# Two convolution-style layers over a 512 x 512 x 128 tensor: products of the first projection one group later, and one reciprocal moved behind a scaling in the second

## The chip, the cores and the metric

The kernel runs on one core of one Trainium2 chip. The metric is the device time of one execution in microseconds (us); lower is better.

## What is computed

The input `x` has 512 x 512 positions of 128 channels in float32. Two layers follow each other, each added to its own input. Cut to what matters here:

```
x = x + L0(group_norm(x))
    a = sigmoid((x @ Wa1 + ba1) * (x @ Wa2 + ba2))      # 16 channels
    b = sigmoid((x @ Wb1 + bb1) * (x @ Wb2 + bb2))      # 16 channels
    z = einsum('bikc,bkjc->bijc', a, b)
    L0 = sigmoid(x @ Wg + bg) * (layer_norm(z) @ Wz + bz)
x = x + L1(group_norm(x))
    xn = layer_norm(x)
    h = (xn @ pi_w.T + pi_b) * sigmoid(xn @ gi_w.T + gi_b) * mask
    a1, b1, a2, b2 = split(h)
    y = concat(einsum('bikd,bjkd->bijd', a1, b1), einsum('bkid,bkjd->bijd', a2, b2))
    L1 = (layer_norm(y) @ po_w.T + po_b) * sigmoid(layer_norm(y) @ go_w.T + go_b)
```

## The kernel before, in words

The program has seven stages that run one after the other; between two stages all engines meet. Stage 1 gathers the statistics of the first group norm, stage 2 computes `a` and `b`, stage 3 multiplies them, stage 4 makes layer 0's output and the second group norm's statistics, stage 5 computes `h`, stage 6 the two products of layer 1, stage 7 its output. The change touches stages 2 and 5.

Every engine has its own written-out order of instructions, and semaphores tie the orders together. No scheduler moves anything: what stands ahead in an engine's order runs ahead.

**Stage 2, the first projection** (`stage2_gates`, lines 388 to 571). The 512 rows of `x` are worked in 128 groups of four rows (1 MB each). Six group buffers are filled ahead by DMA (`load`, line 382). For each group g:

- TensorE turns it, in two halves h of two rows: `turn(r, g, h)`, eight 128 x 128 transposes into one of three slots of `x_ps` (line 454).
- ScalarE scales a half by the group norm and rounds it to fp16: `round_high` writes `high` (line 498). VectorE computes what the rounding left: `rest` writes `low` (line 548). A slot of `x_ps` is free again once `rest` has read it.
- TensorE multiplies with the weights, split in fp16 parts: `product(r, g, m)`, twelve matmuls of 32 x 512 for m = 0 (the first factor) and twelve for m = 1 (the second), into `p_ps[:, m]` (line 467). It waits for both halves of `rest` of its group.
- ScalarE adds the bias to the first factor: `open_first` (line 504). VectorE multiplies in the second: `multiply` writes `gate` (line 555). ScalarE applies the sigmoid: `sigmoid` writes `ab` (line 511). `p_ps` has one buffer for each m, so `product(g, 0)` waits for `open_first(g-1)` and `product(g, 1)` for `multiply(g-1)`.

In one step of the loop, TensorE does turn(g+2, 0), product(g+1, 0), turn(g+2, 1), product(g+1, 1); ScalarE does sigmoid(g), round_high(g+3, 0), open_first(g+2), round_high(g+3, 1); VectorE does multiply(g), rest(g+2, 0), rest(g+2, 1). A body of the loop has six steps, one for each group buffer.

The SP queue issues both loads and stores of this stage: six `reload(r, k)`, each once buffer k has been turned (line 417), and then two `store` of 768 KB, each once the sigmoids of three groups are done (line 421). The second store waits for the sixth sigmoid of the body, and the next body's first load stands behind it in the queue.

**Stage 5, the second projection** (`stage5_project`, lines 995 to 1299). Pairs n of rows are worked, sixteen in a body; eight pairs are a block, whose layer-norm deviations are computed together. For each pair TensorE spreads the reciprocal deviations (`spread_scale`, line 1259), multiplies for the gate and for the projection (`project`, line 1268) and turns the pair n+12 (`turn`, line 1243). VectorE does `scale(n+2)` (line 1194), `statistics(n+11)` (line 1172) and `gate_h(n)` (line 1201). Once in a block ScalarE computes the deviations (`deviation`, line 1084, after pair 4 of the block; it loads an activation table ahead and another after), VectorE inverts them (`invert`, line 1178, in the step of pair 5) and splits the result in two fp16 parts (`split_high`, `split_low`, lines 1183 and 1187), TensorE turns these (`turn_parts`, line 1250), and ScalarE copies the result out (`keep_rows`, line 1089), which the next block's first `spread_scale` needs. The two split steps wait for the reciprocal and for each other by the semaphore `chain`.

Of the kernel before, what the change touches and what calls it, by code (L numbers as in the profile page):

```python
# [387 lines left out]
def stage2_gates(nc, K, ahead, ab_d, N):  # L388
# [11 lines left out]
    with ExitStack() as stack:  # L400
# [12 lines left out]
        def _(block):  # L413
# [25 lines left out]
            @block.tensor  # L439
            def _(pe):  # L440
                for m in range(2):
                    pe.matmul(p_ps[:, m, 0:1], K.Wab4[:, m, :], K.gn_shift[:], start=True, stop=True).then_inc(shifted, 1)
                pe.wait_ge(folded, 2)
                pe.sem_inc(done, 2 * GROUPS)

                def turn(r, g, h):

                    k, n = g % GROUPS, (2 * g + h) % SLOTS
                    if h == 0:
                        pe.wait_ge(loaded[k], (r + g // GROUPS) * 16 + 16)  # L450
                    pe.wait_ge(rest_ready, r * PAIRS + (2 * g + h + 1))
                    for j in range(2):
                        for q in range(CB):
                            last = pe.transpose(x_ps[:, n, j, q * P:(q + 1) * P], xt[:, k, 2 * h + j, q, :], K.ident[:])  # L454
                    last.then_inc(turned, 1)

                def product(r, g, m):
                    pe.wait_ge(rest_ready, r * PAIRS + (2 * g + 2 + SLOTS))
                    if m == 0:
                        pe.wait_ge(opened, r * GROUPS + (g + 1))  # L460
                    else:
                        pe.wait_ge(gated, r * GROUPS + (g + 2))
                    half = slice(32 * m, 32 * m + 32)
                    for weights, part, start, stop in ((K.Wab_high, high, True, False), (K.Wab_low, high, False, False),
                                                       (K.Wab_high, low, False, True)):
                        for j in range(U):
                            last = pe.matmul(p_ps[32 * j:32 * j + 32, m, 0:N], weights[:, half], part[:, g % GROUPS, j, :],
                                             start=start, stop=stop)
                    last.then_inc(done, 1)

                def step(r, g, end=None):
                    for h in range(2):
                        if end is None or g + 2 < end:
                            turn(r, g + 2, h)
                        if end is None or g + 1 < end:
                            product(r, g + 1, h)

                for g in range(2):
                    for h in range(2):
                        turn(0, g, h)  # L480
                for m in range(2):
                    product(0, 0, m)
                with pe.Fori(0, REPS - 1) as r:
                    for g in range(GROUPS):
                        step(r, g)
                for g in range(TAIL):
                    step(REPS - 1, g, TAIL)

            @block.scalar
            def _(act):  # L490
                act.sem_inc(sig, 2)
                act.sem_inc(opened, 1)

                def round_high(r, g, h):
                    act.wait_ge(turned, r * PAIRS + (2 * g + h + 1))
                    if h == 0:
                        act.wait_ge(done, r * PAIRS + (2 * g + 2))
                    act.activation(high[:, g % GROUPS, 2 * h:2 * h + 2, :], x_ps[:, (2 * g + h) % SLOTS, :, 0:N], ACT.Copy,  # L498
                                   scale=K.gn_scale[:]).then_inc(rounded, 1)

                def open_first(r, g):
                    act.wait_ge(done, r * PAIRS + (2 * g + 1 + 2 * GROUPS))
                    act.wait_ge(gated, r * GROUPS + (g + 1))
                    act.activation(first[:, g % 2, :], p_ps[:, 0, 0:N], ACT.Identity, bias=bias[:, 0:1]).then_inc(opened, 1)

                def sigmoid(r, g):
                    k = g % GROUPS
                    act.wait_ge(gated, r * GROUPS + (g + 1 + 2))
                    if k % 3 == 0:
                        act.wait_ge(stored[k // 3], (r + g // GROUPS) * 16 + 16)  # L510
                    act.activation(ab[:, k // 3, k % 3, :], gate[:, g % 2, :], ACT.Sigmoid).then_inc(sig, 1)

                def step(r, g, end=None):
                    sigmoid(r, g)
                    if end is None or g + 3 < end:
                        round_high(r, g + 3, 0)
                    if end is None or g + 2 < end:
                        open_first(r, g + 2)
                    if end is None or g + 3 < end:
                        round_high(r, g + 3, 1)  # L520

                for g in range(2):
                    for h in range(2):
                        round_high(0, g, h)
                act.wait_ge(folded, 2)
                open_first(0, 0)
                round_high(0, 2, 0)
                open_first(0, 1)
                round_high(0, 2, 1)
                act.activation(bias_gate[:], K.bg[:], ACT.Sigmoid)  # L530
                with act.Fori(0, REPS - 1) as r:
                    for g in range(GROUPS):
                        step(r, g)
                for g in range(TAIL):
                    step(REPS - 1, g, TAIL)

            @block.vector
            def _(dve):
                dve.sem_inc(rest_ready, SLOTS)
                dve.sem_inc(gated, 2)  # L540
                for m in range(2):
                    dve.wait_ge(shifted, m + 1)
                    dve.tensor_tensor(bias[:, m:m + 1], p_ps[:, m, 0:1], K.bias4[:, m:m + 1], ALU.add).then_inc(folded, 1)
                dve.wait_ge(folded, 2)

                def rest(r, g, h):
                    dve.wait_ge(rounded, r * PAIRS + (2 * g + h + 1))
                    dve.scalar_tensor_tensor(low[:, g % GROUPS, 2 * h:2 * h + 2, :], x_ps[:, (2 * g + h) % SLOTS, :, 0:N], K.gn_scale[:],  # L548
                                             high[:, g % GROUPS, 2 * h:2 * h + 2, :], ALU.mult, ALU.subtract).then_inc(rest_ready, 1)

                def multiply(r, g):
                    dve.wait_ge(done, r * PAIRS + (2 * g + 2 + 2 * GROUPS))
                    dve.wait_ge(opened, r * GROUPS + (g + 2))
                    dve.wait_ge(sig, r * GROUPS + (g + 1))
                    dve.scalar_tensor_tensor(gate[:, g % 2, :], p_ps[:, 1, 0:N], bias[:, 1:2], first[:, g % 2, :],
                                             ALU.add, ALU.mult).then_inc(gated, 1)

                def step(r, g, end=None):
                    multiply(r, g)
                    if end is None or g + 2 < end:  # L560
                        for h in range(2):
                            rest(r, g + 2, h)

                for g in range(2):
                    for h in range(2):
                        rest(0, g, h)
                with dve.Fori(0, REPS - 1) as r:
                    for g in range(GROUPS):
                        step(r, g)
                for g in range(TAIL):  # L570
                    step(REPS - 1, g, TAIL)

def stage3_triangle(nc, K, ab_d, z_d, N):
# [420 lines left out]
def stage5_project(nc, K, ahead, mask, mask_d, h_d, N):  # L995
# [9 lines left out]
    with ExitStack() as stack:  # L1005
# [27 lines left out]
        def _(block):  # L1033
# [127 lines left out]
            def _(dve):  # L1161
# [14 lines left out]
                def invert(r, b):  # L1176
                    dve.wait_ge(dev_ready, r * 2 + (b + 1))
                    dve.reciprocal(rstd[:], dev[:]).then_inc(chain, 1)
# [24 lines left out]

                def step(r, n, last=False):
                    chained = not (last and n + 3 >= PAIRS)
                    if n % BLOCK == 5 and chained:
                        invert(r, (n + 3) // BLOCK)
                    if not (last and n + 2 >= PAIRS):
                        scale(r, n + 2)
                    if n % BLOCK == 5 and chained:  # L1210
                        split_high(r, (n + 3) // BLOCK)
                        split_low(r, (n + 3) // BLOCK)
                    if not (last and n + LEAD - 1 >= PAIRS):
                        statistics(r, n + LEAD - 1)
                    gate_h(r, n)
# [627 lines left out]
```

## Time and profile before

| what | value |
|---|---|
| median of 3 runs | 4825.3 us (4824.75 to 4827.78) |
| the profiled execution, its own time | 4827.47 us |
| its span, first to last instruction | 4825.7 us |
| mean granted TensorE clock | 0.975 |
| busy: PE, DVE, ACT, POOL | 3997.2, 3925.1, 3395.2, 2674.1 us |
| stage 2: first turn to last sigmoid | 373.9 to 939.3 us |
| stage 5: first turn to last scaling | 2062 to 3142 us |

PE is TensorE's matmuls, PEld its weight loads, DVE VectorE, ACT ScalarE, POOL GpSimd, SPq the queue on which SyncE issues DMAs. A row of a timeline gives start, duration, engine, line, operation, output <- input, and in square brackets how long the engine had been idle before it and what ended that. The busy share of a whole span averages over seven stages with different limits, so it does not say what limits stage 2 or stage 5. Only short stretches inside a stage do.

### The profile page before, as it was taken

The numbers are of one execution on the slowest core, as the hardware profiler recorded it, in microseconds if no ns is written. First come the engines' busy times: TensorE is split into PE (matmuls) and PEld (weight loads), VectorE is DVE, ScalarE is ACT, GpSimd is POOL, SyncE is SP. The second block draws the span as 40 slices with busy tenths as digits, with TensorE's granted clock in tenths as the row PEclk, the third lists the DMA queues.
The fourth block names the chain that finished last, engine by engine and source line by source line (L and its number), as shares of the span: only waits on it lengthen the run. The fifth ranks groups of instructions, "written<-read, shape, count | busy, mean of one in ns | idle before, by whom it ended". The sixth has DMA issues, their size and how long they took to land. (4 is left out here: it accounts for less than half of the span.)

```text
span 4825.7 us, 89597 instructions
## 1 busy us (share of the span) xinstructions
PE 3997.2 (83%) x26438; PEld 2240.6 (46%) x26438; DVE 3925.1 (81%) x5450; ACT 3395.2 (70%) x4840; POOL 2674.1 (55%) x1428
## 2 busy tenths in 40 slices
PE   0007888795599999889999999979999978888888
PEld 0004444452366666545555555545554434444444
DVE  5787777678888888989999999867779987777777
ACT  2337777654577777768888888746667768888887
POOL 0000000085488888757778777843334418888887
PEclk9999999997799999989999999999999989999999
DMA  9997888753999999969999999876679869999999
GB/s 367 416 385 247 296 299 301 241 175 105 307 399 390 390 391 391 393 215 316 315 315 318 311 313 318 276 263 222 224 237 308 302 213 362 407 405 404 402 404 362
DMA packets 700625, 1532.70 MB, mean 318 GB/s; under 512 B 32976, under 2 KB 50832, under 8 KB 698128
## 3 DMA queue, kind: packets, MB, share of 16 engines
q1 hardware_dynamic: 563696, 1263.31, 73.0%
q10 hardware_dynamic: 136864, 268.59, 14.5%
q8 instruction: 33, 0.54, 0.0%
q14 instruction: 32, 0.26, 0.0%
HBM read 1009.59 MB, written 522.19 MB: 317 GB/s over the span
## 5 line engine op out<-in xcount | busy, mean ns | idle before, releaser
L1762 POOL TENSOR_TENSOR s_oT<-s_gated,s7in_x1t 128x1024 f32<-128x1024 f32 x256 | 689.4, 2699 | 218.5 <-DVE s_gated L1681 213.6
L976 POOL TENSOR_TENSOR s_x1T<-s_gz,s_xT 128x512 f32<-128x512 f32 x512 | 653.4, 1276 | 126.6 <-DVE s_gz L942 122.0
L1428 PE MATMUL s_y_ps<-s_ab 128*128 128x512 f16 x3072 | 678.4, 379 | 1.8 <-DVE s_ab L1499 1.8
L1133 POOL TENSOR_TENSOR s_low<-s_xc,s_high 128x1024 f16<-128x1024 f32 x256 | 547.8, 2140 | 237.4 <-ACT s_high L1094 235.9
L873 PE MATMUL s_g_ps<-s_xT,s_Wg 128*128 128x512 f32 x1024 | 523.3, 593 | 0.0
L713 POOL MEMSET s_total<- 128x2048 f32 x1 | 1.8, 1810 | 936.2 <-POOLq L41 936.2
L903 ACT ACTIVATE s_g<-s_g_ps,s_bg 128x512 f32<-128x512 f32 x512 | 352.0, 688 | 173.1 <-PE s_g_ps L873 173.1
L1681 DVE SCALAR_TENSOR_TENSOR s_gated<-s_p_ps,k_po_bias,s_gate 128x1024 f32<-128x1024 f32 x256 | 328.7, 1284 | 177.2 <-ACT s_gate L1718 145.7
L1428 PEld LDWEIGHTS s_y_ps<-s_ab 128*128 128x128 f16 x3072 | 300.4, 98 | 343.4 <-issue 2.0
L548 DVE SCALAR_TENSOR_TENSOR s_low<-s_x_ps,k_gn_scale,s_high 128x1024 f16<-128x1024 f32 x256 | 328.5, 1284 | 161.0 <-ACT s_high L498 160.9
L942 DVE SCALAR_TENSOR_TENSOR s_gz<-s_z_ps,k_z_bias,s_g 128x512 f32<-128x512 f32 x512 | 384.4, 751 | 88.8 <-ACT s_g L903 86.6
L1099 ACT ACTIVATE s_gate<-s_g_ps,k_gi_bias 128x1024 f32<-128x1024 f32 x256 | 284.3, 1110 | 200.7 <-PE s_g_ps L1268 200.4
L1402 POOL TENSOR_TENSOR s_at<-s_at,s_mask 128x1024 f32<-128x1024 f32 x64 | 151.1, 2360 | 460.6 <-DMA s_bt<-h_d 265.6
L1718 ACT ACTIVATE s_gate<-s_g_ps,k_go_bias 128x1024 f32<-128x1024 f32 x256 | 286.0, 1117 | 148.0 <-PE s_g_ps L1627 134.8
L863 PEld LDWEIGHTS s_x_ps<-k_ident,s_xt 128*128 128x128 f32 x2048 | 257.1, 141 | 274.8 <-issue 268.3
L1172 DVE BATCH_NORM_STATS2 s_stats<-s_x_ps 128x6 f32<-128x256 f32 x1024 | 364.1, 418 | 7.8 <-PE s_x_ps L1243 7.1
L1201 DVE SCALAR_TENSOR_TENSOR s_h<-s_p_ps,k_pi_bias,s_gate 128x1024 f32<-128x1024 f32 x256 | 328.2, 1282 | 46.8 <-PE s_p_ps L1268 32.2
L933 DVE BATCH_NORM_STATS2 s_stats<-s_x1T 128x512 f32 (+1 forms) x512 | 349.8, 683 | 0.2 <-POOL s_x1T L976 0.2
L498 ACT ACTIVATE s_high<-s_x_ps,k_gn_scale 128x1024 f16<-128x1024 f32 x256 | 285.2, 1114 | 74.3 <-PE s_x_ps L454 73.6
L307 DVE BATCH_NORM_STATS2 s_stats<-s_xt 128x512 f32 x416 | 248.5, 682 | 81.1 <-DMA s_xt<-in_x 81.1
L863 PE MATMUL s_x_ps<-k_ident,s_xt 128*128 128x128 f32 x2048 | 308.5, 274 | 6.5 <-DVE s_bg L929 6.5
L1194 DVE TENSOR_TENSOR s_xc<-s5in_xt,s_r_ps 128x1024 f32<-128x1024 f32 x256 | 310.2, 1212 | 4.3 <-PE s_r_ps L1259 3.0
(225 smaller groups left out, 9506.7 us busy)
## 6 DMA issues: line engine op xcount, KB each, us to landing
s2in_xt<-in_x SPq DMA_DIRECT2D x128, 1024.0 KB, 8.5
s_xt<-in_x SPq DMA_DIRECT2D x256, 512.0 KB, 8.4
x_d<-s_x1T ACTq DMA_DIRECT2D x128, 1024.0 KB, 9.6
s5in_xt<-x_d SPq DMA_DIRECT2D x128, 1024.0 KB, 9.2
h_d<-s_h SPq DMA_DIRECT2D x128, 1024.0 KB, 6.9
s7in_x1t<-x_d SPq DMA_DIRECT2D x128, 1024.0 KB, 14.0
out<-s_ot ACTq DMA_DIRECT2D x128, 1024.0 KB, 9.3
s_mask_b<-mask_d SPq DMA_DIRECT2D x128, 512.0 KB, 4.8
```

Of the source, the lines that this page charges most:

```text
L548: dve.scalar_tensor_tensor(low[:, g % GROUPS, 2 * h:2 * h + 2, :], x_ps[:, (2 * g + h) % SLOTS, :, 0:N], K.gn_scale[:], high[:, g % GROUPS ...
L863: last = pe.transpose(x_ps[:, i % 4, q * P:(q + 1) * P], xt[:, i // U, i % U, q, :], K.ident[:])
L873: pe.matmul(g_ps[:, i % 2, 0:N], Wg[:], xT[:, i % 8, :], start=True, stop=True).then_inc(g_prod, 1)
L903: act.activation(g[:, i % 2, :], g_ps[:, i % 2, 0:N], ACT.Sigmoid, bias=bg[:]).then_inc(sig, 1)
L933: dve.bn_stats(stats[:, bass.ds(r * ROWS + i, 1), :].rearrange("p a s -> p (a s)"), x1T[:, i // U, i % U, :]).then_inc(counted, 1)
L942: dve.scalar_tensor_tensor(gz[:, i % 4, :], z_ps[:, i % 2, 0:N], K.z_bias[:], g[:, i % 2, :], ALU.add, ALU.mult).then_inc(mixed, 1)
L976: pool.tensor_tensor(x1T[:, i // U, i % U, :], gz[:, i % 4, :], xT[:, i % 8, :], ALU.add).then_inc(added, 1)
L1133: pool.tensor_tensor(low[:, n % 4, :, :], xc[:, n % 4, :, :], high[:, n % 4, :, :], ALU.subtract).then_inc(rest_ready, 1)
L1172: last = dve.bn_stats(stats[:, row // 16 % 2, row % 2, row // 2 % BLOCK, a, :], x_ps[:, row % 2, 2 * a * P:(2 * a + 2) * P].rearrange("p ( ...
L1428: last = pe.matmul(y_ps[:, ib, 0:N], ab[:, u % 2, 0, a, kb, ib * P:(ib + 1) * P], ab[:, u % 2, 1, b, kb, :], start=m == 0, stop=m == len(t ...
L1681: dve.scalar_tensor_tensor(gated[:, n % 4, :, :], p_ps[:], K.po_bias[:], gate[:, n % 2, :, :], ALU.add, ALU.mult).then_inc(mixed, 1)
L1762: pool.tensor_tensor(oT[:, n % 4, :, :], gated[:, n % 4, :, :], x1t[:, n // 2, 2 * (n % 2):2 * (n % 2) + 2, :], ALU.add).then_inc(added, 1)
```

## The change

It has two parts.

In stage 2, TensorE's step becomes turn(g+2, 0), product(g, 0), turn(g+2, 1), product(g, 1): the products belong to a group that is two behind the turned one and not one behind. ScalarE's step becomes round_high(g+2, 0), open_first(g), round_high(g+2, 1), sigmoid(g-1), and VectorE's multiply(g-1), rest(g+2, 0), rest(g+2, 1). The first body of ScalarE and VectorE is written out ahead of their loops, since it has no sigmoid or multiply of an earlier body. The SP queue's order of loads and stores is unchanged.

In stage 5, VectorE does `scale(n+2)` ahead of `invert` in the step of pair 5 of a block, where it did it after.

```diff
@@ stage 2, TensorE
                     for h in range(2):
                         if end is None or g + 2 < end:
                             turn(r, g + 2, h)
-                        if end is None or g + 1 < end:
-                            product(r, g + 1, h)
+                        product(r, g, h)
...
-                for m in range(2):
-                    product(0, 0, m)
@@ stage 2, ScalarE
-                def step(r, g, end=None):
-                    sigmoid(r, g)
-                    if end is None or g + 3 < end:
-                        round_high(r, g + 3, 0)
-                    if end is None or g + 2 < end:
-                        open_first(r, g + 2)
-                    if end is None or g + 3 < end:
-                        round_high(r, g + 3, 1)
+                def step(r, g, first=False, end=None):
+                    ahead = end is None or g + 2 < end
+                    if ahead:
+                        round_high(r, g + 2, 0)
+                    open_first(r, g)
+                    if ahead:
+                        round_high(r, g + 2, 1)
+                    if g:
+                        sigmoid(r, g - 1)
+                    elif not first:
+                        sigmoid(r - 1, GROUPS - 1)
@@ stage 2, VectorE
-                def step(r, g, end=None):
-                    multiply(r, g)
+                def step(r, g, first=False, end=None):
+                    if g:
+                        multiply(r, g - 1)
+                    elif not first:
+                        multiply(r - 1, GROUPS - 1)
                     if end is None or g + 2 < end:
                         for h in range(2):
                             rest(r, g + 2, h)
@@ stage 5, VectorE
-                    if n % BLOCK == 5 and chained:
-                        invert(r, (n + 3) // BLOCK)
                     if not (last and n + 2 >= PAIRS):
                         scale(r, n + 2)
                     if n % BLOCK == 5 and chained:
+                        invert(r, (n + 3) // BLOCK)
                         split_high(r, (n + 3) // BLOCK)
                         split_low(r, (n + 3) // BLOCK)
```

The order of the instructions shows it at three places. On TensorE (the start of stage 2), the 32 transposes of the first two groups stood ahead of the products of group 0, and then came the loop:

```order
 L454 MATMUL s_x_ps<-k_ident,s2in_xt 128x128 x32
-L467 MATMUL s_p_ps<-s_high,k_Wab_high 32x512 x4
-L467 MATMUL s_p_ps<-s_high,k_Wab_low 32x512 x4
-L467 MATMUL s_p_ps<-s_low,k_Wab_high 32x512 x4
-L467 MATMUL s_p_ps<-s_high,k_Wab_high 32x512 x4
-L467 MATMUL s_p_ps<-s_high,k_Wab_low 32x512 x4
-L467 MATMUL s_p_ps<-s_low,k_Wab_high 32x512 x4
-L483 UNCONDITIONAL_BRANCH
```

These six rows of products are gone from there. The loop's rows read the same as before (eight transposes, twelve matmuls, eight transposes, twelve matmuls), but the first twelve matmuls in it are now group 0's and not group 1's.

On ScalarE, one step of the loop in stage 2 (`s_ab` is the sigmoid's output, `s_high` the rounded half, `s_first` the first factor) stood before as

```order
L511 ACTIVATE s_ab<-s_gate 128x512
L495 REGISTER_ALU
L497 REGISTER_ALU
L498 ACTIVATE s_high<-s_x_ps,k_gn_scale 128x1024
L502 REGISTER_ALU
L504 ACTIVATE s_first<-s_p_ps,s_bias 128x512
L498 ACTIVATE s_high<-s_x_ps,k_gn_scale 128x1024
```

and stands now as

```order
L494 REGISTER_ALU
L495 ACTIVATE s_high<-s_x_ps,k_gn_scale 128x1024
L499 REGISTER_ALU
L501 ACTIVATE s_first<-s_p_ps,s_bias 128x512
L495 ACTIVATE s_high<-s_x_ps,k_gn_scale 128x1024
L505 REGISTER_ALU
L508 ACTIVATE s_ab<-s_gate 128x512
```

The sigmoid has moved from the head of a step to its end.

On VectorE in stage 5, in the step of pair 5 of a block (`s_xc` is the scaled pair, `s_rstd` the reciprocal, `s_parts` its two parts, `s_h` the gated projection of the pair before), the order was

```order
L1201 SCALAR_TENSOR_TENSOR s_h<-s_p_ps,k_pi_bias,s_gate 128x1024
L1177 ISA
L1178 RECIPROCAL s_rstd<-s_dev 128x64
L1194 TENSOR_TENSOR s_xc<-s5in_xt,s_r_ps 128x1024
L1181 ISA
L1183 TENSOR_SCALAR s_parts<-s_rstd 128x2x32
L1186 REGISTER_ALU
L1187 SCALAR_TENSOR_TENSOR s_parts<-s_rstd,s_parts 128x2x32
```

and is now

```order
L1206 SCALAR_TENSOR_TENSOR s_h<-s_p_ps,k_pi_bias,s_gate 128x1024
L1199 TENSOR_TENSOR s_xc<-s5in_xt,s_r_ps 128x1024
L1182 ISA
L1183 RECIPROCAL s_rstd<-s_dev 128x64
L1186 ISA
L1188 TENSOR_SCALAR s_parts<-s_rstd 128x2x32
L1191 REGISTER_ALU
L1192 SCALAR_TENSOR_TENSOR s_parts<-s_rstd,s_parts 128x2x32
```

The scaling, which stood between the reciprocal and the first split, stands ahead of both.

## Rows read from the trace of the kernel before

**Rows 1.** Timeline, stage 2: one step's rows on TensorE, ScalarE and VectorE.

```profile
704.33 1.09 PE L454 MATMUL s_x_ps<-k_ident,s2in_xt 128*128 128x128 f32 x8
...
705.46 1.11 ACT L498 ACTIVATE s_high<-s_x_ps,k_gn_scale 128x1024 f16<-128x1024 f32 x1 [0.32 <-PE s_x_ps L454]
...
706.12 1.09 PE L454 MATMUL s_x_ps<-k_ident,s2in_xt 128*128 128x128 f32 x8
...
706.61 1.28 DVE L548 SCALAR_TENSOR_TENSOR s_low<-s_x_ps,k_gn_scale,s_high 128x1024 f16<-128x1024 f32 x1 [1.23 <-ACT s_high L498]
...
707.81 0.74 DVE L555 SCALAR_TENSOR_TENSOR s_gate<-s_p_ps,s_bias,s_first 128x512 f32<-128x512 f32 x1
...
707.95 0.40 PE L467 MATMUL s_p_ps<-s_high,k_Wab_high 128*32 128x512 f16 x4 [0.74 <-DVE s_low L548]
...
708.71 1.09 PE L454 MATMUL s_x_ps<-k_ident,s2in_xt 128*128 128x128 f32 x8
```

**Rows 2.** Timeline, ScalarE at the start of stage 2, where it worked without a wait.

```profile
387.11 0.62 ACT L511 ACTIVATE s_ab<-s_gate 128x512 f32<-128x512 f32 x1
...
390.20 0.63 ACT L511 ACTIVATE s_ab<-s_gate 128x512 f32<-128x512 f32 x1
```

**Rows 3.** Busy time in stretches of stage 2: start:end, length, engines, clock, DMA share, GB/s.

```profile
699.40:722.20 22.80, 19.10 (x215) 11.30 (x208) 16.56 (x17) 17.62 (x22) 0.00 (x0) 1.00 0.99 343
...
705.00:715.00 10.00, 8.52 (x97) 4.88 (x96) 6.67 (x7) 7.80 (x10) 0.00 (x0) 1.00 1.05 392
699.40:725.75 26.35, 21.83 (x244) 13.02 (x240) 18.88 (x19) 20.62 (x25) 0.00 (x0) 1.00 0.86 298
```

**Rows 4.** The same view, a stretch of stage 4.

```profile
1500.00:1550.00 50.00, 50.00 (x233) 31.28 (x232) 44.72 (x67) 38.96 (x67) 42.24 (x34) 1.00 1.04 392
```

**Rows 5.** Timeline, the SP queue in stage 2: three of its load issues.

```profile
709.99 0.37 SPq L382 DMA_DIRECT2D s2in_xt<-in_x  x1
...
714.37 0.37 SPq L382 DMA_DIRECT2D s2in_xt<-in_x  x1
...
725.83 0.40 SPq L382 DMA_DIRECT2D s2in_xt<-in_x  x1
```

**Rows 6.** DMA issues on the page: count, size, median us from issue to landing.

```profile
s2in_xt<-in_x SPq DMA_DIRECT2D x128, 1024.0 KB, 8.5
```

**Rows 7.** Timeline, stage 5: the step with the reciprocal and the next.

```profile
2611.34 0.38 ACT L1084 ACTIVATE s_dev<-s_stats,s_eps 128x64 f32<-128x64 f32 x1
...
2611.75 0.55 DVE L1178 RECIPROCAL s_rstd<-s_dev 128x64 f32<-128x64 f32 x1 [1.20 <-ACT s_dev L1084]
...
2612.22 1.16 DVE L1194 TENSOR_TENSOR s_xc<-s5in_xt,s_r_ps 128x1024 f32<-128x1024 f32 x1
...
2613.30 0.18 DVE L1183 TENSOR_SCALAR s_parts<-s_rstd 128x64 f16<-128x64 f32 x1
...
2613.87 0.23 PE L1250 MATMUL s_r_ps<-k_ident_h,s_parts 128*128 128x128 f16 x1 [0.79 <-DVE s_parts L1187]
2614.05 1.05 ACT L1094 ACTIVATE s_high<-s_xc 128x1024 f16<-128x1024 f32 x1
...
2614.99 0.27 ACT L1089 ACTIVATE s_rows<-s_r_ps 128x128 f16<-128x128 f16 x1
...
2615.72 0.40 PE L1259 MATMUL s_r_ps<-s_rows,s_select 64*128 64x128 f16 x8
...
2616.19 1.22 DVE L1194 TENSOR_TENSOR s_xc<-s5in_xt,s_r_ps 128x1024 f32<-128x1024 f32 x1
...
2620.09 1.22 DVE L1194 TENSOR_TENSOR s_xc<-s5in_xt,s_r_ps 128x1024 f32<-128x1024 f32 x1
```

**Rows 8.** Timeline, stage 5, another block: the turned parts and the next two scalings.

```profile
2314.99 0.23 PE L1250 MATMUL s_r_ps<-k_ident_h,s_parts 128*128 128x128 f16 x1 [1.06 <-DVE s_parts L1187]
...
2317.31 1.22 DVE L1194 TENSOR_TENSOR s_xc<-s5in_xt,s_r_ps 128x1024 f32<-128x1024 f32 x1
...
2322.85 1.22 DVE L1194 TENSOR_TENSOR s_xc<-s5in_xt,s_r_ps 128x1024 f32<-128x1024 f32 x1
```

**Rows 9.** Busy time in a stretch of that block, columns as in Rows 3.

```profile
2317.00:2321.00 4.00, 4.00 (x19) 1.47 (x16) 2.87 (x6) 2.41 (x3) 3.74 (x2) 0.57 0.86 317
```

More of the change, by code:

```diff
@@ L525, in _ @@
                 act.wait_ge(folded, 2)
[L526 to L529, printed above, removed]
                 act.activation(bias_gate[:], K.bg[:], ACT.Sigmoid)
-                with act.Fori(0, REPS - 1) as r:
+                for g in range(GROUPS):
+                    step(0, g, first=True)
+                with act.Fori(1, REPS - 1) as r:
                     for g in range(GROUPS):
@@ L534, in _ @@
                 for g in range(TAIL):
-                    step(REPS - 1, g, TAIL)
+                    step(REPS - 1, g, end=TAIL)
+                sigmoid(REPS - 1, TAIL - 1)
             @block.vector
@@ L566, in _ @@
                         rest(0, g, h)
-                with dve.Fori(0, REPS - 1) as r:
+                for g in range(GROUPS):
+                    step(0, g, first=True)
+                with dve.Fori(1, REPS - 1) as r:
                     for g in range(GROUPS):
@@ L570, in _ @@
                 for g in range(TAIL):
-                    step(REPS - 1, g, TAIL)
+                    step(REPS - 1, g, end=TAIL)
+                multiply(REPS - 1, TAIL - 1)
 def stage3_triangle(nc, K, ab_d, z_d, N):
```

## The prediction

> **What bounds the kernel now.** The page's shares average over seven stages, so I read stretches inside the two stages that the change touches: first the table of busy time, then the timeline, then the queue of the loads.
>
> Stage 2 first. In 26.35 us, one body of six groups, no engine is full: TensorE is busy 21.83 us, ScalarE 20.62, VectorE 18.88, and the DMA engines have a share of 0.86 at a granted clock of 1.00 [rows 3]. A group takes 26.35 / 6 = 4.39 us. Where nothing is full, a loop of waits sets the pace, and the timeline shows it [rows 1]. The second half of a group is turned at 704.33; ScalarE rounds it from 705.46 (1.13 later); VectorE computes the rest from 706.61 (1.15 later); the group's first product waits for just that rest and starts at 707.95 (1.34 later, TensorE idle for 0.74); behind that product the next second half is turned, at 708.71 (0.76 later). 1.13 + 1.15 + 1.34 + 0.76 = 4.38 us, the whole period. So stage 2 is bound by one loop through three engines, closed by the product that stands ahead of the next turn.
>
> Stage 5: a normal step takes 2620.09 - 2616.19 = 3.90 us from scaling to scaling. The step with the reciprocal is longer: from that step's scaling to the next is 2616.19 - 2612.22 = 3.97, but VectorE was idle for 1.20 us ahead of the reciprocal, waiting for ScalarE's deviations, with a scaling that needed nothing behind it, and TensorE idled for 0.79 until the parts were split [rows 7].
>
> **The change, stage 2.** Nothing is added or removed in the work; the same transposes, matmuls, activations and VectorE operations run in another order. A product now needs the rest of a group that was turned a whole step earlier, so the loop above is open. What is next?
>
> - TensorE by itself: a turn and a product take 706.12 - 704.33 = 1.79 us from start to start [rows 1], a group has two of each: 3.57 us.
> - ScalarE: from one sigmoid to the next without a wait 390.20 - 387.11 = 3.09 us [rows 2].
> - VectorE: two rests of 1.20 (706.61 to 707.81) and a multiply of at most 0.74 [rows 1]: 3.14 us.
> - A new loop, over two groups: turn(g+2, 1), rounding, rest; VectorE does multiply(g) behind that rest; product(g+1, 1) waits for it; behind it stand turn(g+4, 0), product(g+2, 0) and the next turn. 1.13 + 1.15 + 1.20 + 0.80 + 0.76 + 1.03 + 0.76 = 6.83 us for two groups, 3.42 for one. It lies 0.31 us over two groups below TensorE's own pace, so it doesn't decide.
> - DMA: a body loads six groups and stores twice 768 KB. The share adds up to 0.99 x 22.80 = 22.6 us of all engines, in a stretch of 22.80 us; the 3.55 us behind it are idle. Where loads alone stand in line the share is 1.05 [rows 3]. If stores and loads fill the engines as well as that, as stage 4 does with loads and stores mixed (1.04 at 392 GB/s [rows 4]), the body needs 22.6 / 1.05 = 21.5 us, 3.59 for a group. If the stretch can't be packed any tighter than it is, it needs 22.8 us, 3.80 for a group.
>
> So the next limit is the DMA between 3.59 and 3.80 us, with TensorE at 3.57 just below. The stores run worse than the loads now, partly since the queue runs dry around them; a closed queue should mend some of it. I take 3.70, the middle, since neither row is nearer. The gain is 4.39 - 3.70 = 0.69 us a group. Of the 128 groups the last two have no turn ahead of them and drain at nearly the old pace, so 126 count: **87 us**. The ends of this term are 126 x (4.39 - 3.80) = 74 and 126 x (4.39 - 3.57) = 103. Filling and draining the pipe by one more group costs at most one product pair, 2 x 0.76 = 1.5 us, and I leave it in the range.
>
> The SP queue is the one that the move lengthens. Its second store waits for the body's sixth sigmoid, which now comes one step later after the turn, and the next body's first load stands behind that store. Buffer 0 of the next body is turned one period behind 714.37, at 718.75 (issues of free buffers come 4.38 apart), and its load is issued at 725.83, 7.1 us later [rows 5]. With 3.70 us a step that becomes about 10.8. The buffer is wanted again six steps after it was free, 22.2 us, so 11.4 us are left for the landing, against a median of 8.5 [rows 6]. It fits, with little to spare, so I cost this at nothing; it is covered only while a landing stays below 11 us.
>
> **Stage 5.** VectorE's scaling fills the 1.20 us of idleness. The reciprocal can't start sooner than 2611.75, since ScalarE's deviation ends then. Behind it the first split needs its result: 0.55 and a semaphore of about 0.07, so it starts at 2612.37 and not at 2613.30, 0.93 us sooner, and the turned parts on TensorE with it. But not all of this reaches the end. The next spreading on TensorE (2615.72) needs ScalarE's copy of the rows, and ScalarE is not early: table, gate and rounding run there without a gap to 2614.99, where the copy starts with no wait [rows 7]. It ends at 2615.26, so the spreading can start at 2615.30, 0.42 us sooner. From there TensorE and VectorE go on at 3.90 a step, TensorE without a gap. 31 blocks pass here (32 reciprocals, one ahead of the loop): 31 x 0.42 = **13 us**. The ends are 31 x 0.93 = 29, if the copy of the rows weren't a brake, and 0, if ScalarE's wait only moves.
>
> **The sum.** 87 + 13 = 100 us off the profiled execution's 4827.5 gives 4727.5. That execution lies 2.2 us above the median, so the forecast is **4725 us**, 2.1% less. Changes within 0.2% (10 us) can hardly be told from none here.
>
> **The rivals.**
> - *TensorE is the bound* (DMA packs to 3.57 or better): 103 + 13, 4709 us. For: 3.59 if loads and stores fill the engines like stage 4. Against: each body's first load is issued late. Chance 0.20.
> - *The DMA can't be packed tighter*: 3.80 a group, 74 + 10, 4741 us. For: stores run at a lower rate than loads whatever stands behind them. Chance 0.18.
> - *The clock falls once in every body*: with 3.70 us of DMA against 3.57 of TensorE, 6 x 0.13 = 0.8 us of waiting collect in front of one turn. At 1.64 us for each of 21 bodies, all of it on the path: 34 us given back, 4759 us. Against: a late TensorE has DMA slack to catch up with. Chance 0.05. This is what the rule above would make of it.
> - *The order doesn't open the loop*: something on ScalarE, whose open_first(g) stands ahead of round_high(g+2, 1), delays the rounding as before; the two-group loop would have to grow from 6.83 to 8.78 us. Then only stage 5 gains: 4812 us. Chance 0.03.
> - *Slower*: the late second store starves the loads. It decides where a body's first load lands more than 6 x 4.39 - (7.1 + 4.4) = 14.8 us after its issue. If landings double to 17 us the body takes 17 + 11.5 = 28.5 us, 4.75 a group: 126 x 0.36 = 45 us more, less 13, 4857 us. Against: the landing of 8.5 us is already that of a queue with three in line. Chance 0.04.
>
> **How the numbers follow.** The forecast's own case, 3.62 to 3.78 a group, has 0.50. The low end takes in TensorE as the bound and some of stage 5's upper end (4709 less 9), the high end the rival on the clock: 4700 to 4762. All of stage 2's better cases lie in it; outside are the last two and a stage 2 worse than 3.85, about 0.12. Faster by over 0.2% are the first three and the forecast, 0.94 with the share of the fourth that is below 4815; slower 0.04; within 0.2% 0.02.
>
> **What would show it.** In the profile after, a stretch of six groups in stage 2 should last 22.2 us, with a DMA share above 1.0 and no idle stretch, the product's wait for the rest gone and instead one wait a body for a load on TensorE. TensorE at 3.57 with DMA share below 1.0 would speak for the first rival, a share near 0.99 at 22.8 for the second, a granted clock below 1.00 in stage 2 for the third. In stage 5 the wait ahead of the reciprocal should shrink to almost nothing, the one for the split parts too, and the copy of the rows should be what the spreading waits for. A stage 2 above 4.2 us a group, or a stage 5 that isn't shorter, would make the reasoning wrong.

## The result, and the profile after

The changed kernel takes 4711.9 us (median of 4 runs, 4710.5 to 4714.6), the kernel before 4826.0 in the same comparison: a ratio of 0.9762, 95% interval 0.9750 to 0.9775, so 2.4% or 114 us less. The forecast was 4725 us with a range of 4700 to 4762. The direction and the range hold; the time is that of the first rival (4709 us), TensorE as the bound of stage 2.

| | before | after | difference |
|---|---|---|---|
| the profiled execution, its own time | 4827.5 | 4714.6 | -112.9 |
| span | 4825.7 | 4712.9 | -112.8 |
| stage 2, first to last sigmoid | 387.1 to 938.7 | 391.1 to 840.1 | -102.6 |
| stage 5, first to last scaling | 2087.1 to 3140.7 | 1988.0 to 3024.3 | -17.3 |

The two stages account for 119.9 us; the rest moved by 7 us the other way. 3.5 us of it lie ahead of stage 2's first turn (at 373.9 us before and 377.4 after), in a stage that the change doesn't touch, and 3.6 us behind stage 5. The kernel with only stage 5 changed (below) has its first turn at 377.3 too, so the first part belongs to the executions and not to the change.

Stage 2 in the busy-time view of the profile after, columns as in [rows 3]: one body of the loop, from a first load's issue to the next body's.

```profile
647.02:668.44 21.42, 21.42 (x243) 13.01 (x242) 18.88 (x19) 19.95 (x25) 0.00 (x0) 1.00 1.02 367
```

A body takes 21.42 us and not 26.35, a group 3.57. TensorE is busy in all of it (this view counts as busy the 0.1 to 0.2 us between two kinds of matmuls that are looked at below), the clock is at 1.00 and the DMA engines have a share of 1.02 at 367 GB/s. The timeline of one step, TensorE and VectorE and ScalarE, answers to [rows 1]:

```profile
700.16 1.09 PE L454 MATMUL s_x_ps<-k_ident,s2in_xt 128*128 128x128 f32 x8
...
700.73 1.28 DVE L547 SCALAR_TENSOR_TENSOR s_low<-s_x_ps,k_gn_scale,s_high 128x1024 f16<-128x1024 f32 x1
...
701.18 0.40 PE L467 MATMUL s_p_ps<-s_high,k_Wab_high 128*32 128x512 f16 x4
...
701.94 1.09 PE L454 MATMUL s_x_ps<-k_ident,s2in_xt 128*128 128x128 f32 x8
...
702.44 1.28 DVE L547 SCALAR_TENSOR_TENSOR s_low<-s_x_ps,k_gn_scale,s_high 128x1024 f16<-128x1024 f32 x1 [0.42 <-ACT s_high L495]
...
702.97 0.40 PE L467 MATMUL s_p_ps<-s_high,k_Wab_high 128*32 128x512 f16 x4
...
703.73 1.09 PE L454 MATMUL s_x_ps<-k_ident,s2in_xt 128*128 128x128 f32 x8
```

From turn to turn of the same half 703.73 - 700.16 = 3.57 us. The products at 701.18 and 702.97 follow their turns with no wait; the 0.74 us ahead of the first product in [rows 1] are gone, and VectorE's wait for the rounding is 0.42 us where it was 1.23.

The load issues of the SP queue answer to [rows 5], and the landing on the page to [rows 6]:

```profile
656.68 11.11 SPq L422 DMA_DIRECT2D ab_d<-s_ab  x2
668.44 8.63 SPq L382 DMA_DIRECT2D s2in_xt<-in_x  x6
```

```profile
s2in_xt<-in_x SPq DMA_DIRECT2D x128, 1024.0 KB, 9.6
```

A merged row runs from its first issue to its last. The six loads of a body are now issued within 8.6 us, and a load of this stage lands 9.6 us after its issue in the median (8.5 before). The first of them is the one that its buffer waits for longest. The sixth goes out as soon as its own buffer is turned, at 676.3; the first buffer was turned five groups of 3.57 us earlier, so the load at 668.44 is issued some 10 us after its buffer came free. TensorE has no wait for a load in the waits of this stretch, so this late issue is covered.

Stage 5, the step with the reciprocal, answers to [rows 7]:

```profile
2405.69 1.21 DVE L1199 TENSOR_TENSOR s_xc<-s5in_xt,s_r_ps 128x1024 f32<-128x1024 f32 x1
...
2406.97 0.55 DVE L1183 RECIPROCAL s_rstd<-s_dev 128x64 f32<-128x64 f32 x1
...
2407.56 0.43 DVE L1188 TENSOR_SCALAR s_parts<-s_rstd 128x64 f16<-128x64 f32 x1
...
2408.38 0.23 PE L1254 MATMUL s_r_ps<-k_ident_h,s_parts 128*128 128x128 f16 x1
...
2409.26 1.05 ACT L1099 ACTIVATE s_high<-s_xc 128x1024 f16<-128x1024 f32 x1
...
2410.21 0.27 ACT L1094 ACTIVATE s_rows<-s_r_ps 128x128 f16<-128x128 f16 x1
...
2410.53 0.40 PE L1263 MATMUL s_r_ps<-s_rows,s_select 64*128 64x128 f16 x8 [0.23 <-ACT s_rows L1094]
2439.59 0.55 DVE L1183 RECIPROCAL s_rstd<-s_dev 128x64 f32<-128x64 f32 x1
```

The scaling runs where VectorE was idle, and the reciprocal starts with no wait as soon as the deviations are there. From it to the turned parts are 1.41 us (2.12 before), but the spreading that begins the next block now waits for ScalarE's copy of the rows, which stands behind the rounding as it did. This block takes 2439.59 - 2406.97 = 32.62 us, as most do; the mean from 2080.56 to 2831.79 is 32.66, over 23 blocks. Before, a block without a fall of the clock took 33.03 (reciprocals at 2611.75 and 2644.78 in the trace of before).

### The profile page after: what moved, and what is told of

Read it like the earlier page. It is cut to its first block and busy times, and to the rows that moved or that the text cites. A ratio compares the mean times of both kernels' runs of the same rounds, so it can differ in the third digit from the quotient of the medians.

```text
span 4712.9 us, 89415 instructions
## 1 busy us (share of the span) xinstructions
PE 3987.0 (85%) x26438; PEld 2239.9 (48%) x26438; DVE 3935.2 (83%) x5450; ACT 3377.8 (72%) x4840; POOL 2670.3 (57%) x1428
## 5 line engine op out<-in xcount | busy, mean ns | idle before, releaser
L1199 DVE TENSOR_TENSOR s_xc<-s5in_xt,s_r_ps 128x1024 f32<-128x1024 f32 x256 | 311.7, 1218 | 10.8 <-PE s_r_ps L1263 9.6
```

## The experiments

Eight more kernels ran, three of them once only: the two with fewer products and the one with the sigmoid at the head. The comparisons with the kernel before were made in three sets, in which its own median was 4826.0, 4828.1 and 4829.6 us, so differences between sets are good to some 4 us.

**One part of the change at a time.** Stage 5's edit undone:

```diff
+                    if n % BLOCK == 5 and chained:
+                        invert(r, (n + 3) // BLOCK)
                     if not (last and n + 2 >= PAIRS):
                         scale(r, n + 2)
                     if n % BLOCK == 5 and chained:
-                        invert(r, (n + 3) // BLOCK)
                         split_high(r, (n + 3) // BLOCK)
```

> The changed kernel with stage 5's scaling put back behind the reciprocal. If the two parts add up as the stages' lengths in the two traces say (stage 2 102 us shorter, stage 5 17 us shorter), it takes 4826 - 102 = 4724 us, a group of stage 2 takes 3.57 us, and stage 5's blocks take 33.03 us again, with a wait of 1.2 us ahead of each reciprocal and again a few falls of the clock. If stage 5's gain came from somewhere else (less heat or another phase after a shorter stage 2), it stays near 4712 us.

Measured: 4728.3 us, a ratio of 0.9791 (0.9776 to 0.9806), 99.8 us less than before and 4 more than expected. Stage 2 is as in the changed kernel (448.9 us from first to last sigmoid, 449.0 there). The waits of the middle of stage 5 in this kernel's trace (engine, line, waited for, total us, times, longest):

```profile
DVE s_rstd L1183 <- ACT s_dev L1089: 33.5, 28, 1.2
PE s_r_ps L1255 <- DVE s_parts L1192: 21.8, 28, 0.8
```

The 1.2 us ahead of each reciprocal are back, 28 times, and blocks take 33.02 us again. But the granted clock was 1.00 through all of the middle of stage 5: the falls of [rows 8, 9] did not come back with the wait. TensorE's wait was at most 0.8 us here. In the trace of before, the three blocks with a fall were those where it had waited longer, 1.06, 1.27 and 1.17 us, and the others had 0.76 to 0.79.

The other half alone, the kernel before with only stage 5's edit:

```diff
-                    if n % BLOCK == 5 and chained:
-                        invert(r, (n + 3) // BLOCK)
                     if not (last and n + 2 >= PAIRS):
                         scale(r, n + 2)
                     if n % BLOCK == 5 and chained:
+                        invert(r, (n + 3) // BLOCK)
                         split_high(r, (n + 3) // BLOCK)
```

> The kernel before with only stage 5's scaling moved ahead of the reciprocal. Theory (ScalarE's copy of the rows limits a block to 0.41 us of gain, and the three falls of the clock at 1.6 us each vanish with the wait): 31 x 0.41 + 5 = 18 us less, 4808 us, blocks of 32.62 us, granted clock 1.00 in the middle of stage 5. Rival (the falls of the clock are chance and come back): 13 us less, 4813 us, with clock below 1.00 in some blocks.

Measured: 4815.6 us, a ratio of 0.9974 (0.9964 to 0.9984), 12.5 us less. The rival's number, 31 x 0.41 = 13, is the right one: the 5 us of the three falls are not in the difference of the medians. The traces agree. From first to last scaling, stage 5 took 1053.6 us in the trace of before, with three falls, but 1048.6 and 1049.6 us with the same order of stage 5 in the kernel with only stage 2 changed (no fall) and in the kernel before with fewer products (one fall); with the new order it is 1037.5 us here and 1036.3 in the changed kernel. How many falls the other executions of the kernel before had, no trace shows. There was no fall in this trace's middle either, so what the rival said of the clock did not show. The two halves add: 99.8 + 12.5 = 112.3 us, against 114 for both.

**Which loop bound stage 2 before.** The kernel before with the third of a product's matmul passes left out. The low part of the input is then computed and not multiplied.

```diff
-                    for weights, part, start, stop in ((K.Wab_high, high, True, False), (K.Wab_low, high, False, False),
-                                                       (K.Wab_high, low, False, True)):
+                    for weights, part, start, stop in ((K.Wab_high, high, True, False), (K.Wab_low, high, False, True)):
```

> The kernel before with the same third matmul pass left out in stage 2. Theory of one loop through turn, rounding, rest and the first product: only one of the two products lies in the loop, so the group falls by 0.215 us, from 4.39 to 4.17: 28 us less, 4798 us. Rival, TensorE's own pace sets the period with waits as a by-product: it falls by 0.43, 55 us less, 4771 us. Rival, the DMA sets it: no change.

Measured: 4802.3 us, 25.8 less than before. First to last sigmoid took 524.7 us where it took 551.6: 26.9 us over 127 groups, 0.21 a group. TensorE lost 0.43 us of work in a group and the group got 0.21 shorter: one product lies in the loop, the other beside it. That is the loop of the prediction, and neither rival. The run cut both products at once; that it is the first one that lies in the loop is read from [rows 1], where TensorE waits ahead of that one.

**What is next in stage 2: TensorE or the DMA.** The same edit on the changed kernel.

> The changed kernel with the third of the three matmul passes of a product in stage 2 left out (the low part of the input is computed but not multiplied), so TensorE's own work in a group falls by 2 x 0.215 = 0.43 us to 3.14. If TensorE is the bound with the DMA clearly below it, the group falls to 3.20 us (the loop over two groups, 6.83 - 0.43, is then the longest): 128 x 0.37 = 47 us less, about 4665 us. If the DMA is right behind TensorE (3.43 us at its full share), the group falls only to 3.43 and the time by 18 us to about 4694 us, with a DMA share of 1.05 and waits of TensorE for loads.

Measured: 4691.8 us, 20 less than the changed kernel. Busy time in stage 2 of this kernel:

```profile
600.00:700.00 100.00, 93.06 (x936) 57.31 (x934) 92.98 (x89) 93.45 (x118) 0.00 (x0) 1.00 1.04 382
```

and its longest waits of a stretch of 250 us there that name a DMA or TensorE's products:

```profile
PEld s_p_ps L466 <- DVE s_gate L553: 27.9, 72, 1.4
...
ACT s_ab L507 <- DMA ab_d<-s_ab: 14.1, 11, 2.3
```

With 0.43 us of TensorE's work gone, a group gets only some 0.16 us shorter: three bodies take 716.42 - 655.03 = 61.39 us by their first loads' issues, 3.41 us a group. No engine is full now, and the DMA has its full share of 1.04. Other than expected, the wait doesn't show at the loads. It shows at ScalarE's sigmoid, which waits for a store to land before it can write its buffer again; VectorE and the products queue up behind it. So the DMA stands at 3.41 us, right behind TensorE's 3.57. That it is the rate and not the landing time of a store is argued from the share of 1.04; no kernel with fewer bytes ran.

**Half of the new order.** The changed kernel with ScalarE's sigmoid at the head of a step, where it stood before.

```diff
                 def step(r, g, first=False, end=None):
                     ahead = end is None or g + 2 < end
+                    if g:
+                        sigmoid(r, g - 1)
+                    elif not first:
+                        sigmoid(r - 1, GROUPS - 1)
                     if ahead:
                         round_high(r, g + 2, 0)
                     open_first(r, g)
                     if ahead:
                         round_high(r, g + 2, 1)
-                    if g:
-                        sigmoid(r, g - 1)
-                    elif not first:
-                        sigmoid(r - 1, GROUPS - 1)
```

> The changed kernel with ScalarE's sigmoid at the head of its step in stage 2, where it stood before, while the products stay a group later. Theory: a new loop closes in one group: multiply(g), 0.79, sigmoid(g), 0.52, round_high(g+3, 0), 1.01, open_first(g+1), 0.57, round_high(g+3, 1), 1.15, rest(g+3, 1), 1.20, multiply(g+1): 5.24 us a group, against 3.57 in the changed kernel and 4.39 in the kernel before: 4712 + 128 x 1.67 = 4926 us, slower than the kernel before. Rival: the place of the sigmoid is of no weight, since ScalarE has 0.5 us of slack a group: 4712 us.

Measured: 4922.9 us, 211 more than the changed kernel and 93 more than the kernel before. The timeline of one step:

```profile
600.66 0.63 ACT L508 ACTIVATE s_ab<-s_gate 128x512 f32<-128x512 f32 x1 [2.01 <-DVE s_gate L554]
...
601.20 1.10 ACT L495 ACTIVATE s_high<-s_x_ps,k_gn_scale 128x1024 f16<-128x1024 f32 x1
...
602.20 0.68 ACT L501 ACTIVATE s_first<-s_p_ps,s_bias 128x512 f32<-128x512 f32 x1
...
602.76 1.11 ACT L495 ACTIVATE s_high<-s_x_ps,k_gn_scale 128x1024 f16<-128x1024 f32 x1
...
603.91 1.28 DVE L547 SCALAR_TENSOR_TENSOR s_low<-s_x_ps,k_gn_scale,s_high 128x1024 f16<-128x1024 f32 x1 [0.30 <-ACT s_high L495]
605.11 0.74 DVE L554 SCALAR_TENSOR_TENSOR s_gate<-s_p_ps,s_bias,s_first 128x512 f32<-128x512 f32 x1
605.89 0.63 ACT L508 ACTIVATE s_ab<-s_gate 128x512 f32<-128x512 f32 x1 [2.01 <-DVE s_gate L554]
```

From sigmoid to sigmoid 5.23 us: sigmoid, rounding, opening, rounding, rest, multiply, and the next sigmoid, each behind the other. ScalarE is idle for 2.01 us ahead of the sigmoid, with two roundings behind it whose input is long there. Each step of this chain is cheap, and ScalarE works 3.2 us of the 5.23; the order alone makes it the longest loop of the kernel. So moving the products is worth 102 us only together with moving the sigmoid.

**A version that beats both.** TensorE's gaps: in the changed kernel a turn takes 1.02 us to the start of the product behind it (700.16 to 701.18), but the eight weight loads of its transposes only 0.86. A product takes 0.76 us to the next turn (701.18 to 701.94), but its twelve matmuls, at 0.215 us for each four, only 0.645. The two products of a step put side by side:

```diff
                     for h in range(2):
                         if end is None or g + 2 < end:
                             turn(r, g + 2, h)
-                        product(r, g, h)
+                    for m in range(2):
+                        product(r, g, m)
...
                     if ahead:
                         round_high(r, g + 2, 0)
+                        round_high(r, g + 2, 1)
                     open_first(r, g)
-                    if ahead:
-                        round_high(r, g + 2, 1)
```

> The changed kernel with the two turns of a step and then its two products on TensorE, and both roundings ahead of the opening on ScalarE. In the trace after, a turn takes 1.02 us from start to start of the product and a product 0.76 to the turn behind it, though eight transposes are 0.86 and twelve matmuls 0.645; the rest is a weight load that waits at each switch. If the gaps belong to the switch, two of four go, about 0.28 us a group, and ScalarE at 3.09 isn't yet the bound: 3.3 us a group, 35 us less than the changed kernel, 4677 us, unless the DMA (3.43 at its full share) stops it at 18 us less, 4694 us. If the gaps belong to each turn and product whatever stands behind it, nothing changes, 4712 us.

Measured: 4694.5 us, a ratio of 0.9721 (0.9706 to 0.9736), 17 us less than the changed kernel. Its stage 2:

```profile
600.84 1.97 PE L454 MATMUL s_x_ps<-k_ident,s2in_xt 128*128 128x128 f32 x16
...
602.73 0.40 PE L467 MATMUL s_p_ps<-s_high,k_Wab_high 128*32 128x512 f16 x4
...
603.39 0.39 PE L467 MATMUL s_p_ps<-s_high,k_Wab_high 128*32 128x512 f16 x4
```

```profile
600.00:700.00 100.00, 96.55 (x1156) 65.35 (x1144) 90.44 (x87) 92.21 (x116) 0.00 (x0) 1.00 1.04 379
```

```profile
ACT s_ab L509 <- DMA ab_d<-s_ab: 12.6, 12, 2.0
```

From the first product to the second are 0.66 us and not 0.76, and the sixteen transposes take 1.89 us to the first product, 0.87 more than eight did; so the gap belongs to the switch. First to last sigmoid is 431.9 us where the changed kernel has 449.0, 17 us less. TensorE has gaps again while the DMA share is 1.04, and ScalarE's sigmoid waits for a store to land as it did in the kernel with fewer products (the last row, from a stretch of 250 us), which needs 429.0 us: the gain stops where that one stopped.

In stage 5, the copy of the rows ahead of the rounding on ScalarE:

```diff
+                    if n % BLOCK == 5 and not (last and n + 3 >= PAIRS):
+                        keep_rows(r, (n + 3) // BLOCK)
                     if not (last and n + 2 >= PAIRS):
                         round_high(r, n + 2)
                     if n % BLOCK == 4 and not (last and n + 4 >= PAIRS):
                         deviation(r, (n + 4) // BLOCK)
-                    if n % BLOCK == 5 and not (last and n + 3 >= PAIRS):
-                        keep_rows(r, (n + 3) // BLOCK)
```

> The changed kernel with ScalarE's copy of the rows ahead of the rounding in the step of pair 5 of a block of stage 5. If that copy is what the next spreading waits for (0.23 us of waiting in the matmul's row, 0.5 us in the weight load's), a block gets 0.3 us shorter, 31 x 0.3 = 9 us: 4703 us. If the rounding, now 0.2 us later, is needed as soon, the gain is given back: 4712 us or more.

Measured: 4707.1 us, a ratio of 0.9749 (0.9735 to 0.9762), 5 us less than the changed kernel, between the two expectations and hardly clear of the scatter between sets; in the traces, first to last scaling is 1030.0 us against 1036.3. The wait for the copy is gone from the trace, and another has come:

```profile
DVE s_h L1206 <- ACT s_gate L1104: 19.0, 45, 0.7
```

In the changed kernel that wait was 2.2 us in all. From reciprocal to reciprocal, blocks last between 32.33 and 32.86 us, and 32.48 in the mean (2083.48 to 2830.53, 23 blocks), 0.18 less than in the changed kernel: some of them get the 0.3 us and others lose them again. That the gate's new wait is what takes them back was not tried. That the copy was what the spreading waited for is shown; that it was worth 9 us is not.

Both edits together:

> The changed kernel with both of the last edits, the adjacent products of stage 2 and the early copy of the rows of stage 5. If they are independent, their gains add: 9 us beside whatever the adjacent products give, 4668 to 4685 us.

Measured: 4688.2 us, a ratio of 0.9709 (0.9696 to 0.9723), the fastest of all, 24 us less than the changed kernel, where the two edits alone gave 17 and 5, and 6 us less than the adjacent products in the same set. So the gains add, within the scatter. It lies 3 us above the upper end of what was expected, since the copy brings less than 9.

## Why the prediction was right, and what was off, point by point

- **What bound stage 2** was right in size and place. The loop of turn, rounding, rest and first product gave 4.38 us, and taking 0.215 us out of each product took 0.21 out of the group and not 0.43, as it must where only one product lies in the loop.
- **What comes next** was the weak step. "I take 3.70, the middle": the group takes 3.57, TensorE's own pace, which the list had right at 3.57. The forecast's own case, 3.62 to 3.78 a group with a chance of 0.50, did not come; a rival with 0.20 did, and the total stayed in the range because the range took that rival in. Of the signs that were named, a body takes 21.42 us and not 22.2, and TensorE has no wait for a load. The rival's own sign, a DMA share below 1.0, is not met either: the share is 1.02 with TensorE full. That TensorE is the bound is shown by its full busy time and by the two kernels that take work or gaps from it and get 20 and 17 us faster.
- **The term for the DMA** was mis-sized. It was 3.59 to 3.80 and measures 3.41. Its error was to add up the busy share as if it were work: 22.6 us of share in a body of [rows 3]. The same 7.86 MB (six loads of 1.05 MB, two stores of 0.79) took 1.02 x 21.42 = 21.8 us of share after the change and 1.04 x 20.5 = 21.3 with fewer products, so the share per byte falls when the queue closes. The bytes over the rate of stage 4, where loads and stores are mixed too, 7.86 MB / 392 GB/s = 20.1 us or 3.34 a group [rows 4], would have been the nearer bound, and by it the first rival the forecast.
- **The sum** of stage 2 was 87 us; it is 102. 126 x (4.39 - 3.57) = 103 stood in the prediction as the upper end and is what was measured.
- **The late second store**, costed at nothing with 11.4 us for the landing, was right: the first load is issued some 10 us after its buffer came free (10.8 in the prediction), the median landing is 9.6 us and TensorE waits for no load. But that was a matter of 2 us.
- **Stage 5** was 13 us with the copy of the rows as the brake; the kernel with that edit alone has 12.5, and a block 0.41 us of the 0.42 worked out. In the trace stage 5 is 17.3 us shorter, since the profiled execution of before also had three falls of the clock, worth 5 us.
- **The rule on the clock** did not come into play. Nowhere in stage 2 does TensorE wait for a load, so the Trainium skill's case ("TensorE: Matmul & The Clock Gate", "HAM oscillation — how this bites in real kernels") had no occasion, and no run here shows what a wait per body would do. The prediction took from [rows 8, 9] that one wait of 1.06 us can be followed by a fall. The traces show that, but not that such a wait suffices. In the kernel before with fewer products, the wait of the same matmul was 1.38 us ahead of one fall, and 1.11 and 1.14 us in two other blocks with the clock at 1.00 behind them. In stage 2 of the kernel with adjacent products, TensorE waited three times for a load, up to 0.8 us, and ten times for VectorE's rest, up to 1.3 us, with the clock at 1.00 throughout.
- **The slower rival** named the wrong place. An order that is slower than before lies close by, but on ScalarE: the sigmoid left at the head of its step costs 211 us. The prediction had the loop over two groups and not this one, which could be worked out from the same rows.

## What to carry to other kernels

Where no engine is full, follow one item around until the chain closes on itself, and add up the starts; then do the same for the order that is proposed, on every engine, since a wait at the head of one engine's step can close a new loop that is longer than the old one. For what the DMA will bound once the loop is open, divide the bytes by the rate of a stretch that is full with loads and stores mixed (here that came within 2%), and don't scale a busy share. The profile of one execution may hold events, such as a fall of the clock, that its median doesn't; a gain read from them should be kept out of the sum.

## What the runs showed of the hardware

- The DMA engines' busy share for the same bytes is no constant: 22.6, 21.8 and 21.3 us of share for 7.86 MB at 298, 367 and 382 GB/s.
- In stage 2 a switch on TensorE between the fp32 transposes (tile 128*128) and the fp16 products (tile 128*32) costs a gap even without a wait: 0.16 us from transposes to matmuls, and 0.10 back, where twelve matmuls take 0.66 us to the next twelve and 0.76 to a transpose behind them. The type alone does not make it. In stage 5 of the changed kernel, two fp16 matmuls of tile 128*128 take 0.43 us to the transposes behind them, their own rate of 0.215 each, so there is no gap; these eight transposes take 0.97 us to the matmuls of tile 64*128 behind them, where stage 2 has 1.02. Whether the tile's shape is what costs the time was not tried.

```profile
2403.82 0.59 PE L1272 MATMUL s_p_ps<-s_low,k_Wpi 128*128 128x512 f16 x2
2404.25 1.04 PE L1247 MATMUL s_x_ps<-k_ident,s5in_xt 128*128 128x128 f32 x8
2405.22 0.40 PE L1263 MATMUL s_r_ps<-s_rows,s_select 64*128 64x128 f16 x8
```

- The granted clock fell in the middle of stage 5 four times in two traces, each time behind a longer wait of the same matmul: 1.06, 1.27 and 1.17 us in the kernel before, 1.38 in the kernel before with fewer products. None came behind waits of 0.8 us or less, of which the kernel before has 27 and the one with only stage 2 changed the 28 of the row shown above, and none in that stretch of the seven traces in which the reciprocal stands behind the scaling, but none came behind two waits of 1.11 and 1.14 us either. So a longer wait went ahead of each fall and was not enough for one; what else decides stays open.
